# A causal mask moved from matmuls to a select on GpSimd, in a four-layer kernel on one core

## The reference, cut to what matters

```
L0:  x = x + attention(x[0], ctx[0])                  # 16 heads, batch element 0 only, added to all
L1:  x = mamba2(x);  x = x + cross(ln(x), ctx) @ Wo   # 8 heads, padding mask
L2:  x1 = ln(x  + mha(x, x, causal=True))             # 16 heads of 16 channels, token mask
     x2 = ln(x1 + mha(x1, ctx, causal=False))
     x  = ln(x2 + fc2(relu(fc1(x2))))
L3:  h  = ln(x + attention(q=x, k=ctx, causal=True))  # 16 heads of 16 channels
     out = gelu(h @ W1.T + b1) @ W2.T + b2 + h

causal:  energy = where(key > query, -inf or -1e9, energy);  p = softmax(energy)
```

## Time and profile before

| | us |
|---|---|
| median of 3 runs (lowest to highest) | 1675.93 (1673.30 to 1677.19) |
| profiled execution, its own time | 1673.93 |
| span of its profile | 1672.1 |
| TensorE busy (share of the span) | 1609.6 (96%) |
| VectorE | 1387.7 (83%) |
| ScalarE | 1073.6 (64%) |
| GpSimd | 494.2 (30%) |

### The profile page before, as it was taken

How to read it: one execution, slowest core, us unless ns; L and a number is a source line. 1 busy time by engine, 2 the same in 40 slices (tenths; PEclk the granted TensorE clock), 3 DMA queues, 4 the chain that set the end, 5 groups by cost and what they waited for, 6 DMA issues and landing times.

```text
span 1672.1 us, 61077 instructions
## 1 busy us (share of the span) xinstructions
PE 1609.6 (96%) x24963; PEld 1383.7 (83%) x24963; DVE 1387.7 (83%) x3587; ACT 1073.6 (64%) x2797; POOL 494.2 (30%) x1256
## 2 busy tenths in 40 slices
PE   7889999999999999999999999999999999999886
PEld 6777888888888888888888888888888888888774
DVE  4588888888888889888888988888898888888552
ACT  2356666766666676666667666666766666676552
POOL 1333223333322332332233233223323322332110
PEclk9999999999999999999999999999999999999997
DMA  6120001000000000000000000000000000000000
GB/s 208 43 81 21 5 19 31 18 25 28 21 2 25 24 25 25 25 22 4 25 24 25 24 24 23 4 24 25 25 24 25 16 10 24 22 28 18 5 5 7
DMA packets 31316, 44.36 MB, mean 27 GB/s; under 512 B 3008, under 2 KB 26176, under 8 KB 30912
## 3 DMA queue, kind: packets, MB, share of 16 engines
q1 hardware_dynamic: 31040, 40.46, 7.6%
HBM read 36.12 MB, written 4.33 MB: 24 GB/s over the span
## 4 chain that ended last, share of the span: by engine, by line
PE 56%; DVE 35%; issue 5%; POOL 2%; DMA 1%; ACT 1%; DVEq 0%; SPq 0%; POOLq 0%; ACTq 0%
PE ring L639 20%; PE ring L645 14%; PE ring L627 6%; DVE conv L1363 5%; DVE maxima_at L1261 5%; PE score L707 4%; DVE decay L1397 3%; PE score L731 3%; PE ring L773 3%; DVE conv L1369 2%; PE ring L858 2%; DVE decay L1401 2%; DVE QB L1272 2%; DVE conv L1358 2%; PE score L671 2%
## 5 line engine op out<-in xcount | busy, mean ns | idle before, releaser
L1538 POOL TENSOR_TENSOR stat<-stat 128x1 f32<-128x1 f32 x224 | 131.7, 594 | 612.8 <-DVE stat L1227 612.3
L1019 ACT COPY actT<-ring 128x256 f32<-128x256 f32 x256 | 95.5, 373 | 264.6 <-PE ring L627 264.2
L1261 DVE TENSOR_REDUCE maxima_at<-score 128x4 f32<-128x512 f32 x388 | 240.8, 684 | 26.0 <-PE score L707 25.2
L1052 ACT ACTIVATE weights<-score 128x512 f32<-128x512 f32 x388 | 200.6, 607 | 28.6 <-PE score L731 28.1
L1363 DVE SCALAR_TENSOR_TENSOR conv<-raw,vectors,conv 128x128 f32<-128x128 f32 x576 | 169.2, 349 | 6.8
L639 PE MATMUL ring<-actT,w_q 128*128 128x128 f32 x1024 | 141.4, 281 | 0.7 <-ACT actT L1019 0.7
L639 PEld LDWEIGHTS ring<-actT,w_q 128*128 128x128 f32 x1024 | 124.5, 191 | 12.8 <-issue 11.3
L639 PE MATMUL ring<-actT,w_up 128*128 128x128 f32 x1024 | 129.1, 280 | 0.5 <-ACT actT L1019 0.5
L639 PEld LDWEIGHTS ring<-actT,w_up 128*128 128x128 f32 x1024 | 120.6, 194 | 3.7 <-ACT actT L1019 1.1
L731 PE MATMUL score<-QB,KE 32*128 32x128 f32 x3104 | 116.7, 286 | 3.8 <-issue 2.8
L1187 ACT ACTIVATE gT<-ring,vectors 128x128 f32<-128x128 f32 x256 | 73.0, 368 | 70.3 <-PE ring L639 69.6
(11 more groups left out here) (179 smaller groups left out, 3809.7 us busy)
## 6 DMA issues: line engine op xcount, KB each, us to landing
decay<-rates_out SPq DMA_DIRECT2D x32, 512.0 KB, 4.1
cT<-in_ctxT SPq DMA_DIRECT2D x32, 128.0 KB, 2.2
x_in<-in_x SPq DMA_DIRECT2D x32, 128.0 KB, 2.5
out<-result SPq DMA_DIRECT2D x32, 128.0 KB, 2.1
row_all<-in_rows SPq DMA_DIRECT2D x1, 1420.0 KB, 10.2
w_in<-in_in_proj SPq DMA_DIRECT2D x1, 1288.0 KB, 6.5
w_k<-in_k SPq DMA_DIRECT2D x4, 256.0 KB, 7.4
w_v<-in_v SPq DMA_DIRECT2D x4, 256.0 KB, 7.2
```

The source lines that it names most:

```text
L1019: nc.scalar.copy(dst.rearrange("p c k -> p (c k)"), t[:, 0:n]).then_inc(read, 1)
L1052: run(weights[:, turned_buffer(it, a_, l), r, :], score[:, r, :], ACT.Exp).then_inc(S["exps"], 1)
L1261: nc.vector.tensor_reduce(maxima_at[:, maxima_buffer(it, a_, l), 32 * r:32 * (r + 1)].rearrange("p (f s) -> p s f", f=2)[:, 0:DC, :], scor ...
L1538: tt(stat[:, l, 10:11], stat[:, l, 2:3], stat[:, l, 4:5], ALU.pow).then_inc(S[done], 1)
```

## The change

`quadsT` of attentions 2 and 4 no longer lays the mask. Its first matmul in each bank now starts the bank itself, as in attention 3. The exponentials are taken of all keys, later ones included. Then a new task of GpSimd, `kept2` or `kept4`, goes over the four tiles of `weights`: it waits for each tile's exponential and sets the entries with key later than query to zero, in place, by an `affine_select`. `values` of these attentions waits for the selects instead of the exponentials. `quads` lays its mask as before, since the maxima are to be taken over allowed keys only; the second half of the mask, its load and its conversion go.

All the numbers of TASKS, FIRST, LAST, SETUP and SHIFT are new, with entries for kept2 and kept4. Of TASKS and of SHIFT for GpSimd a line or two stand here for the rest.

```diff
 TASKS = dict(
-    spread=22.7901, store=23.1605, turn1=32.8102, uT=26.5226, up0=66.8312, up1=67.8745, values1=33.4323, values2=42.004,
...
+    V1=22.8357, V2=40.5446, V3=49.8726, V4=53.6033, Wo=36.937, Y=27.5829, am=3.0085, kept2=44.0231, kept4=66.9201,
...
+    up0=69.2927, up1=70.2809, values1=36.1471, values2=45.2921, values3=53.0084, values4=65.6731, x1=16.0514, x1r=15.56,
...
-        n2=-0.0248, n3=2.0304, norm5=3.5039, proj=0.6654, softplus=1.1659, uT=-0.0221, x1r=1.4386, z0=1.9558),
...
+        kept2=-0.3071, kept4=-2.4418, n2=-0.2543, n3=1.1113, norm5=2.4581, proj=1.4014, uT=0.1861, x1r=1.4656, z0=4.017),
...
+CAUSAL = (2, 4)
...
+KEPT = [unit for unit in TURNED if unit[0] in CAUSAL]
+assert KEPT == [(int(task[-1]), l, i) for task, l, i in ORDER["POOL"] if task.startswith("kept")]
...
+def kept_done(it, a_, l, n):
+
+    return TILES * it.number(KEPT_AT, a_, l) + n + 1
...
-        causal_bf = sb("causal_bf", [P, 2, TILES, P], BF16)
+        causal_bf = sb("causal_bf", [P, TILES, P], BF16)
...
-                sp.dma_start(dx[:, :, :].rearrange("p m n -> p (m n)"), a["masks"]).then_inc(S["later_in"], 16)
+                sp.dma_start(dx[:, 0, :], a["masks"]).then_inc(S["later_in"], 16)
...
             def quadsT(it, a_, l):
 
-                masked = a_ in (2, 4)
                 evacuated(it, f"mT{a_}", l)
                 if a_ in (2, 3):
                     pe.wait_ge(S[f"KE{a_}"], nth(it, l))
-                if masked:
-                    lay_causal(it, "quadsT", a_, l, 1)
                 for c in range(DC):
                     for e in range(2):
                         at = (2 * c + e) * P
                         for r, rows_of in enumerate(ROWS_OF):
-                            if not masked and at == 0:
+                            if at == 0:
                                 free(it, "quadsT", a_, l, r)
                             last = mm(score[:, r, at:at + P], KE[rows_of, l, c, e, :], QB[rows_of, l, c, e, :],
-                                      start=(not masked and at == 0), stop=(c == DC - 1 and e == 1))
+                                      start=(at == 0), stop=(c == DC - 1 and e == 1))
...
             def values(it, a_, l):
 
                 output, full = claim(it, f"values{a_}", l)
-                pe.wait_ge(S["exps"], exps_done(it, a_, l, TILES - 1))
+                if a_ in CAUSAL:
+                    pe.wait_ge(S["kept"], kept_done(it, a_, l, TILES - 1))
+                else:
+                    pe.wait_ge(S["exps"], exps_done(it, a_, l, TILES - 1))
...
-                    ts(causal_bf[:, :, :, :], dx[:, :, :].rearrange("p m (q k) -> p m q k", q=TILES), MASKED, None, ALU.mult)
+                    ts(causal_bf[:, :, :], dx[:, 0, :].rearrange("p (q k) -> p q k", q=TILES), MASKED, None, ALU.mult)
...
+                def not_later(a_, l):
+
+                    for r in range(TILES):
+                        wait_for(S["exps"], exps_done(it, a_, l, r))
+                        heads = weights[:, turned_buffer(it, a_, l), r, :].rearrange("p (h k) -> p h k", k=P)
+                        nc.gpsimd.affine_select(heads, heads, [[0, DC * 2], [1, P]], ALU.is_ge, 0.0, base=0,
+                                                channel_multiplier=-1).then_inc(S["kept"], 1)
...
-                          x1r=power("seed1", "rstd1"))
+                          x1r=power("seed1", "rstd1"), kept2=lambda l: not_later(2, l), kept4=lambda l: not_later(4, l))
```

More of the change, by code:

```diff
@@ L50 @@
 TASKS = dict(
[L51 to L58, removed]
@@ new lines @@
+    K1=30.3087, K2=38.7749, K3=48.003, K4=53.5587, KE2=34.7183, KE3=55.6514, Q1=32.5787, Q2=39.1867, Q3=48.4552, Q4=58.8384,
+    V1=22.8357, V2=40.5446, V3=49.8726, V4=53.6033, Wo=36.937, Y=27.5829, am=3.0085, kept2=44.0231, kept4=66.9201,
+    attT2=47.5531, attT3=23.2356, attT4=57.2406, back2=45.473, back3=53.2718, back4=66.6942, conv0=17.1479, conv1=0.6915,
+    ctxT=36.6395, decayed=35.4015, down=73.7705, dt=6.9786, e2=40.2174, e3=50.1271, exps2=50.0532, exps3=12.3387,
+    exps4=23.5235, fc1=55.4143, fc2=56.5825, finish1=-6.7846, finish2=45.8478, finish3=51.6708, finish4=65.9348, ld=23.8563,
@@ new lines @@
+    loadc=23.7736, loadx=-11.2028, mT2=42.5161, mT3=51.2652, mT4=63.0087, n2=41.6919, n3=51.3553, norm2=36.3525, norm3=25.4909,
+    norm4=40.5443, norm5=66.6616, pairs=23.9195, proj=29.2847, quads1=33.1101, quads2=40.2601, quads3=49.184, quads4=59.9676,
+    quadsT2=43.0343, quadsT3=51.7372, quadsT4=64.3988, row=47.2364, scan=15.6471, scores1=33.9288, scores2=33.6927,
+    scores3=49.3722, scores4=70.4545, silu=23.3048, softplus=21.4364, spread=25.9829, store=13.403, turn1=34.7737, uT=28.9593,
@@ L195 @@
[L195 to L203 removed]
+        K0=7.4185, K2=-0.3928, K4=-0.0996, KE2=4.2652, KE3=-6.6038, Q0=1.0686, Q1=0.1147, Q2=0.055, V0=-4.3462, V1=0.1751,
@@ new lines @@
+        V3=-0.2945, Y=0.6743, attT0=1.1297, attT2=-2.7982, attT3=29.7117, attT4=8.245, ctxT=-0.5788, exps0=-1.1049,
+        exps2=-7.3281, exps3=39.7601, exps4=41.1644, ld=-0.0603, prep_in=6.085, row=-0.0661, scores1=0.0828, silu=0.0116,
+        softplus=-0.8703, turn1=-0.0393, uT=-0.4592, up0=0.0069, up1=-0.2422, x2T=0.1156, x3T=-0.0166, x4T=-0.3146,
+        x5T=-0.3779, x6T=-0.3504, xbc0=0.0645, xbc1=0.2298, xhatT=-0.0765, xnT=0.0757, z0=0.0649),
+    DVE=dict(
+        K1=0.6768, K3=0.3507, V4=1.1002, Wo=0.9334, Y=0.9234, conv0=3.8008, conv1=22.3729, decayed=-7.3068, down=1.2144,
+        e2=1.2861, e3=0.7847, fc2=0.938, finish0=0.0593, finish1=43.5456, finish2=0.2543, finish3=2.7077, finish4=1.7808,
+        mT0=8.983, mT2=0.7221, mT3=0.637, mT4=0.7701, n2=1.2966, n3=1.2438, norm2=9.865, norm3=29.5473, norm4=17.4911,
+        norm5=1.3674, pairs=0.8702, prep_in=0.3861, prep_masks=1.7156, prep_out=0.6452, prep_q1=-5.1432, proj=1.2442,
+        scan=11.662, scores0=-27.4981, scores1=0.1301, scores2=8.5394, scores3=0.4245, scores4=-9.288, silu=1.2585,
+        softplus=-0.1637, uT=0.8633, x1=0.3494, x1r=1.2716, xhat=-13.9005, xnT=-0.2801),
```

276 lines of the change are left out of this document (128 added, 148 removed).

## The result

The changed kernel takes **1818.54 us** (median of 4 runs, 1814.6 to 1819.08) beside 1674.62 us for the kernel before on the same chip: ratio 1.0863, 95% interval 1.0822 to 1.0905. It is 8.6% slower. The prediction said 1772 us with a range of 1660 to 1890: the time lies in the range and the sign is right, but the cost was put at 98 us where 144 were measured.

The account below looks back on a forecast made before the run. A two-leg chain per element, 25.7 us on TensorE then 23.0 on VectorE, was taken as the bound. Terms -0.36 + 1.25 + 0.95 + 0.15 + 1.2 = 3.2 us, 30 periods: 1673.9 + 96 + 1.7 = 1772 us, range 1660 to 1890.

Parts of the forecast that it names:

- The masks: Mask matmuls dropped on TensorE: -0.36 us per element before quadsT2, 0 before quadsT4, which lies beside VectorE's leg.
- rival A: The masks' TensorE time is simply won, both groups paying: 23 us saved, 1651 us; chance 0.17.
- The price of one select: Time of one GpSimd select over 128x512, called c: 0.75 us, ends 0.61 and 1.50.
- rival C: A GpSimd select costs what its tensor_scalar costs, 1.5 us: 7.4 to 9.4 us per element, 1898 to 1957 us; chance 0.13.
- values2 waits for the selects: TensorE stands before values2 until four GpSimd selects end: 4c - 1.74, +1.25 us per element, ends 0.7 and 4.25.
- My sign for it: Check in the new profile: if values2 doesn't wait, or waits above 3 us, the assumed select cost is wrong.
- back2 behind attT: With back2 right behind values2, TensorE waits for ScalarE's copy attT: +0.95 us per element.
- Selects beside the convolution: GpSimd's kept4 selects hold up VectorE's conv1 passes: +1.2 us per element, ends 0 and 2.2.
- DVE's order: Moved VectorE steps around the maxima of quads3: +0.8 us in front, -0.65 behind, together +0.15 per element.
- TensorE's clock: Less busy TensorE gets a lower granted clock (0.93 seen): up to 1.8 us per period, added only in rival C.
- Rival B: The order alone eats the gain, cheap selects missing conv1: 0.74 us per element, 1698 us, or 1674 with VectorE's slack; chance 0.18.
- values4's cover: x2T's wait in front of values4 hides its wait for kept4: 0 up to c about 0.9, then 4 us per us.

Follow-up runs that it names:

- experiment 7: Changed kernel with Q4 and xnT put back between values2 and back2 on TensorE, as before; 1817.56 us, 146.0 above the kernel before.
- experiment 4: Changed kernel with the selects run on a scratch tile nobody reads and values waiting for the exponentials; 1790.21 us, ratio 1.0723 to the kernel before.
- experiment 1: Kernel before with the change's new order alone, both masks still laid by TensorE, no select; 1774.62 us, ratio 1.0625.
- experiment 12: Kernel before with one number changed: z0's two GpSimd passes moved behind the root of attention 3's norm; 1705.46 us, ratio 1.0202.
- experiment 8: experiment 1 with Q4, xnT and z0 moved back, mT4 in front of K3, VectorE's softplus behind quads3's maxima; 1757.29 us, ratio 1.0524.

## Why the prediction was right in sign and range, and short in size

The change, taken apart by these runs: +104 us for the order, +56 for the selects in that order, -16 for the masks.

- **The masks**, -0.36 us per element, 11 us: right in kind, 15.8 measured. That all 23 us could be won (rival A) is out.
- **The price of one select**, c = 0.75 with ends 0.61 and 1.50: 0.674 us on average, and 2.59 for four in a row. The split of the two-input row was nearer than the one-input row, and C's price is out.
- **values2 waits for the selects**, +1.25: not in the changed kernel. Two estimates missed by a little: the selects run back to back, without my 0.07 between them, and TensorE reaches values2 10.3 us behind Y's start, where I had 9.6. With 2.59 for the four selects my sum still has a wait of 0.5; the 0.7 by which TensorE comes later takes that away. My sign for it (no wait, so c is wrong) pointed at the wrong term. Where Q4 is taken away from in front of it the wait is there, 1.19 us (experiment 7).
- **back2 behind attT**, +0.95: 0.84 in the profile and on the chain, but not to be added to the term above: taking it away brings the other one (experiment 7, +146.0 against +143.9).
- **Selects beside the convolution**, +1.2: (209.9 - 169.2) us over 32 elements is 1.27, and experiment 4 shows that such a loss counts in full.
- **DVE's order**, +0.15. **This is the step that failed.** With back2's term I had 1.1 us per element for the order, 33 us; the order alone costs 104 (experiment 1), some 3.5 per element. The profile of experiment 1 says where: in the first leg I had 1.75 more (0.95 and 0.8) and 2.3 were measured; in the second I had 0.65 less and 1.2 more were measured. I weighed the moves on VectorE around the maxima of quads3 and left out moves on other queues. z0 went behind the root of attention 3's norm on GpSimd, beside VectorE's scan and decay step: 0.77 us per element on line 1400, and 0.76 instead of 0.48 us for the pass in front of the scan (line 1236 of experiment 1 at 902.72, beside z0's first pass). That is most of the second leg's 1.2, and the move costs 33.5 us in the kernel before (experiment 12). turn1 went in front of quads3 on TensorE (0.87 us, seen in experiment 8). The steps in front of the maxima cost more than I took: from VectorE's K step at 901.69 to the maxima 5.24 us. What else lengthens the first leg is not taken apart move by move, and experiment 8 shows that three of the moves alone do not carry the 104.
- **TensorE's clock**, which I had put into rival C alone: it came in the forecast's own case, behind a wait of 1.3 us. 13 to 16 us come back with four fillers. The forecast had nothing for it.
- **Rival B** (the order alone decides) named the largest part, with 22 us for it instead of 104.
- **Smaller slips in the sums**, none of which moves the forecast: the wait of values2 is 4c - 1.77 by its own terms, not 1.74; B without back2's 0.95 comes to 1669, not 1674; values4's cover ends at a c of about 0.8, not 0.9, so that c = 1.1 adds 1.2 there and not 0.4.

The sum was nearer than its terms, and that was luck: a wait of values2 (38 us in the sum) that did not come stood in for a part of an order that cost 70 us more.

In experiment 12 z0's pass gets done only behind the scan (1.06 us after its end), and the decay step only behind z0's pass (1.08 us after its end). The Trainium skill (SBUF — State Buffer, Who interferes with whom) has VectorE's second SBUF input come through an interface that GpSimd's reads share, taken for a whole instruction. These rows come near that rule: whole passes would be 1.34 and 1.22 us. By it the selects' term beside the convolution would be 2.2 us per element and the sum 1802. I had taken 1.2, and 1.27 was measured. For the select the change's profile shows less than the rule: GpSimd is at its four selects from 911.97 to 914.53, beside nine passes of line 1362 that take 4.15 us (start 910.79) instead of 2.71. That is 1.44 of 2.56 us.

No version here beats the kernel before. The cheapest use of a select, attention 2 alone in the old order, is 3.3% slower.

## What to carry to other kernels

A new order is many changes: list for every engine what moved past what, GpSimd's long two-input passes above all, and ask which VectorE step with two SBUF inputs they now run beside. Two waits in a row on one engine may not add up: here the one for the selects was hidden behind Q4, and taking away the one at back2 brought it out, so price the pair. Work handed to another engine needs a free place in that engine's queue at that moment: four selects of 0.65 us per element cost 167 us where they stood behind a softplus chain (attention 4), and 57 us where only two roots stood in front (attention 2, with n2 moved and values2 started in halves).

## What was not expected of the hardware

TensorE's granted clock fell to 0.51, about the lower of its two levels (1.2 and 2.4 GHz), in a period in which it was busy for 50.7 of 54.5 us. The fall came right behind stretches in which it was busy for 1.78 of 3.00 and 1.57 of 2.00 us. Elements in which quadsT3 fell into it took 1.5 to 1.9 us longer (54.45 and 54.79 against 52.9). Four matmuls that compute nothing made the kernel 13 to 16 us faster; eight made it no faster.
